# Latent attention: the causal mask and the row maximum of the scores in one VectorE pass per head

## The reference

```python
cq = _rmsnorm(x @ Wq_down, gq)
Q = (cq @ Wq_up).reshape(B, S, H, dh).transpose(0, 2, 1, 3)
Q_nope, Q_rope = (Q[..., :nope], Q[..., nope:])
...
KV_lora = _rmsnorm(KV_lora, gkv)
KV = (KV_lora @ Wkv_up).reshape(B, S, H, dh + nope).transpose(0, 2, 1, 3)
...
mask = jnp.where(jnp.tril(jnp.ones((S, S), jnp.float32)) == 1, 0.0, -1000000000.0)
scale = 1.0 / jnp.sqrt(jnp.float32(q_heads.shape[-1]))
scores = jnp.einsum('bhsd,bhtd->bhst', q_heads, k_heads) * scale + mask
attn = jax.nn.softmax(scores, axis=-1)
out = jnp.einsum('bhst,bhtd->bhsd', attn, V)
out = out.transpose(0, 2, 1, 3).reshape(B, S, D) @ Wo
```

## Time and profile before

| | |
|---|---|
| median of 3 runs | 3078.67 us (3078.39 to 3084.72) |
| the profiled execution | 3087.53 us |
| its span in the trace | 3086.1 us |
| latent stage in it | 0 to about 562 us |
| TensorE busy over the span | 2887.0 us (94%) |
| VectorE busy over the span | 2055.0 us (67%) |
| mean granted TensorE clock | 0.967 of full speed |

### The profile page before, as it was taken

How to read it: one execution, slowest core, us unless ns; L and a number is a source line. 1 busy time by engine, 2 the same in 40 slices (tenths; PEclk the granted TensorE clock), 3 DMA queues, 4 the chain that set the end, 5 groups by cost and what they waited for, 6 DMA issues and landing times.

```text
span 3086.1 us, 46590 instructions
## 1 busy us (share of the span) xinstructions
PE 2887.0 (94%) x16712; PEld 1971.4 (64%) x16745; DVE 2055.0 (67%) x3792; ACT 1595.0 (52%) x2971; POOL 1138.1 (37%) x1152
## 2 busy tenths in 40 slices
PE   8899998899998889999996999999999999989998
PEld 3344443444443548888865888888888888856665
DVE  3554445699986877777776445656555566549998
ACT  2223222288887537777752444444456455437764
POOL 2343243334422033333345445454544444323310
PEclk9899999799999889999997999999999999989999
DMA  3000000000000238865673013222122234120000
GB/s 132 1 1 1 1 1 1 8 6 6 3 2 21 80 139 331 326 247 192 213 222 98 21 32 84 63 57 68 49 90 88 81 115 134 35 89 8 15 15 21
DMA packets 125913, 238.83 MB, mean 77 GB/s; under 512 B 14283, under 2 KB 73248, under 8 KB 119285
## 3 DMA queue, kind: packets, MB, share of 16 engines
q1 hardware_dynamic: 102020, 119.95, 12.1%
q0 software_dynamic: 22512, 113.80, 10.7%
q10 hardware_dynamic: 1152, 2.10, 0.2%
HBM read 223.99 MB, written 40.63 MB: 86 GB/s over the span
## 4 chain that ended last, share of the span: by engine, by line
PE 55%; DVE 13%; issue 7%; ACT 6%; POOL 3%; DMA 1%; SPq 0%; POOLq 0%; ACTq 0%; DVEq 0%; another core or an unknown queue 0%
PE ps L1651 9%; PE ps L1653 9%; PE ps L1652 9%; PE ps L901 3%; PE ps L890 3%; PE ps L2918 2%; DVE ps L2493 2%; PE ps L879 2%; PE ps L2928 2%; DVE b_mx L1023 1%; PE ps L2893 1%; ACT d_PTh L2355 1%; PE ps L1665 1%; ACT d_qk L2340 1%; DVE d_PTl L2507 1%
## 5 line engine op out<-in xcount | busy, mean ns | idle before, releaser
L2693 POOL TENSOR_SCALAR d_P<-d_P,d_rv 128x128 f32<-128x128 f32 (+3 forms) x256 | 289.8, 1144 | 553.2 <-DVE d_rv L2500 552.9
L1023 DVE TENSOR_REDUCE b_mx<-ps 128x1 f32<-128x512 f32 x512 | 320.8, 683 | 31.7 <-PE ps L879 28.1
L964 ACT ACTIVATE b_PT<-ps 128x512 f32<-128x512 f32 x512 | 277.6, 601 | 45.0 <-PE ps L890 43.5
L2348 ACT ACTIVATE d_P<-ps,d_nb 128x128 f32<-128x128 f32 (+3 forms) x256 | 135.2, 528 | 219.0 <-DVE d_nb L2493 217.7
L2507 DVE TENSOR_TENSOR d_PTl<-ps,d_PTh 128x384 fp32r<-128x384 f32 (+1 forms) x192 | 114.6, 597 | 157.4 <-ACT d_PTh L2355 157.4
L1651 PE MATMUL ps<-d_xh,d_wh 128*128 128x512 f32 x512 | 210.1, 410 | 1.5 <-DVE d_xl L2467 1.4
L1652 PE MATMUL ps<-d_xl,d_wh 128*128 128x512 f32 x512 | 204.1, 399 | 0.0
L1653 PE MATMUL ps<-d_xh,d_wl 128*128 128x512 f32 x512 | 203.9, 398 | 0.0
L879 PE MATMUL ps<-b_KT,b_Q 64*128 64x512 f32 x512 | 201.0, 475 | 2.1 <-DVE b_mx L1023 1.0
L890 PE MATMUL ps<-b_Q,b_KT 64*128 64x512 f32 x512 | 187.1, 452 | 0.5
L476 ACT ACTIVATE a_P<-ps 128x2048 f32<-128x2048 f32 (+1 forms) x48 | 76.4, 1592 | 210.0 <-PE ps L340 183.0
(11 more groups left out here) (485 smaller groups left out, 8456.3 us busy)
## 6 DMA issues: line engine op xcount, KB each, us to landing
eoscr<-x_eo SPq DMA_DIRECT2D x87, 256.0 KB, 4.3
d_w<-in_L_attn_W_Q SPq DMA_DIRECT2D x32, 256.0 KB, 3.9
d_w<-in_L_attn_W_K SPq DMA_DIRECT2D x32, 256.0 KB, 4.7
d_w<-in_L_attn_W_V SPq DMA_DIRECT2D x32, 256.0 KB, 5.4
d_wo<-in_L_attn_W_O SPq DMA_DIRECT2D x16, 512.0 KB, 4.7
d_cmb<-in_wgT SPq DMA_DIRECT2D x16, 512.0 KB, 5.0
d_cmb<-in_wuT SPq DMA_DIRECT2D x16, 512.0 KB, 4.7
d_cmb<-in_wdT SPq DMA_DIRECT2D x16, 512.0 KB, 4.2
```

The costliest lines, as they stand in the source:

```text
L964: e.activation(M.PT[:, half, v % 2, 2 * p + y, :], ps[:, O.bank(("ex", v, y)), :], ACT.Exp, scale=0.25).then_inc(S["b_ex"], 1)
L1023: e.tensor_reduce(M.mx[:, r % 2, q, h:h + 1], ps[:, O.SCORES[O.score(t, h) % 3], :], AX.X, ALU.max).then_inc(S["b_mx"], 1)
L2693: e.tensor_scalar(P, P, M.rv[:, y, q:q + 1], None, ALU.mult).then_inc(S["d_nm"], 1)
```

## The change

In `scores` the mask matmuls (L322) are gone, 256 in all; those of `turned` stay. VectorE no longer takes the maximum of four heads by one reduction: for each head and block, one `tensor_tensor_reduce` adds a mask from SBUF (`M.mk`: 384 columns of zero, then the 128x128 mask, so that its last w columns fit a block of w columns), writes the sum back to PSUM and gives the maximum. A group has 16 of them in place of 4 reductions. `M.mk` is filled once at the start, on VectorE. Part 1 now begins with the small block.

```diff
@@ scores
         for q, c0 in (((3, 0),), ((2, 0), (0, 384)), ((1, 0),))[j]:
             w = 128 * (q + 1)
             for i in range(4):
-                e.matmul(ps[:, i, c0:c0 + w], M.QT[32 * i:32 * i + 32, c, q * 128:q * 128 + 128], M.KT[32 * i:32 * i + 32, c, 0:w], start=True, stop=False)
-            for i in range(4):
-                t = e.matmul(ps[:, i, c0 + w - 128:c0 + w], G.identb, G.maskb, start=False, stop=True)
+                t = e.matmul(ps[:, i, c0:c0 + w], M.QT[32 * i:32 * i + 32, c, q * 128:q * 128 + 128], M.KT[32 * i:32 * i + 32, c, 0:w], start=True, stop=True)
         t.then_inc(S["a_S"], 1)
@@ peak
-        if j == 1:
-            e.tensor_reduce(M.mx[:, 0, :], ps[:, 0:4, 384:512], AX.X, ALU.max)
-        q = 3 - j
-        w = 128 * (q + 1)
-        e.tensor_reduce(M.mx[:, q, :], ps[:, 0:4, 0:w], AX.X, ALU.max).then_inc(S["a_mx"], 1)
+        if g == 0 and j == 0:
+            e.wait_ge(S["a_mk"], 2)
+        for q, c0 in (((3, 0),), ((0, 384), (2, 0)), ((1, 0),))[j]:
+            w = 128 * (q + 1)
+            for i in range(4):
+                part = ps[:, i, c0:c0 + w]
+                t = e.tensor_tensor_reduce(out=part, in0=part, in1=M.mk[:, 512 - w:512], scale=1.0, scalar=-3.4e38, op0=ALU.add, op1=ALU.max,
+                                           accum_out=M.mx[:, q, i:i + 1])
+        t.then_inc(S["a_mx"], 1)
@@ latent_dve, at the start
             t.then_inc(S["cb"], 1)
+            e.memset(M.mk[:, 0:384], 0.0).then_inc(S["a_mk"], 1)
+            e.tensor_copy(M.mk[:, 384:512], G.cst[:, C_MASK:C_MASK + 128]).then_inc(S["a_mk"], 1)
```

More of the change, by code:

```diff
@@ L189, in latent_memory @@
     M.rec, M.o = sb("a_rec", [128, 512]), sb("a_o", [128, 4, 512])
+    M.mk = sb("a_mk", [128, 512])
     return M
```

## The result

| | before | after |
|---|---|---|
| median of 6 runs each, taken together | 3084.48 us (3078.39 to 3094.44) | 3096.84 us (3092.36 to 3101.42) |
| ratio to before | | 1.0043, 95% interval 1.0031 to 1.0055 |
| span of the profiled execution | 3086.1 us | 3093.0 us |
| last matmul of the latent stage | 563.0 us | 573.7 us |
| TensorE busy over the span | 2887.0 us | 2881.0 us |

The change makes the kernel slower by 0.43%, about 13 us; 4.8 were forecast. All of it arises in the latent stage, which ends 10.7 us later in the profiled execution. The later stages of that execution gave 3.8 us back, nearly all of it between 2755 and 3069 us (times of the kernel before), where TensorE was equally idle in both (17.7 and 17.8 us) and had 12.9 us at the lower clock instead of 19.9. The last row of the table is summed from the trace's clock records.

What follows compares the result with a forecast made beforehand. The latent stage was taken as bound by the chain of scores, maximum, turned and exponential, not TensorE alone. Chain +0.3 us plus clock 4.5 gave +4.8 on 3078.67, so 3083.5 us, range 3075 to 3085.

Steps and rivals of the forecast that it cites:

- the sum: Latent stage: gains and costs at 45 places where turned follows a maximum, +0.3 us; with 4.5 us for TensorE's clock, +4.8.
- TensorE's clock: Lower clock behind longer idle time before turned, part 1, of groups 5, 9, 13: +4.5 us, ends 0 and 9.
- kind C: 20 places where fill work covers the maximum and turned begins without idle time; the scores' earlier end is won: -7.9 us.
- The price of a pass: VectorE: passes of 512, 384, 256, 128 columns 0.66, 0.53, 0.38, 0.26 us apart; maxima longer by 0.44, 0.90, 0.39 us.
- rival of full reads and tails: Every accumulator read and pass tail on VectorE counts in full: +26 us, with the clock +30, 3109 us; chance 0.13.
- Kind B: Six places, part 1 of groups 3 to 13 (odd), where VectorE starts the maximum late; its added length costs +5.4 us.
- kind A: 17 places where VectorE follows the scores at once and turned follows the maximum at once: +1.9 us.
- m: How much earlier scores end without mask matmuls: 0.33 us in parts 0 and 2, 0.66 us in part 1.
- D: Two places, part 1 of groups 14 and 15, with VectorE and TensorE nearly even: +0.9 us.
- rival of a clock that falls more often: TensorE's clock falls at more than three places and stays low longer: +0.3 + 9 us, 3088 us; chance 0.17.
- period over 134 us: Test on the time of four groups, expected 130 to 132 us; above 134 the price of a pass would be wrong.

Runs made afterwards that it cites:

- e4_settle_behind: Changed kernel with the settling of the group before moved on VectorE from ahead of the maximum of part 1 to behind it: 3077.00 us, ratio 0.9980 to before.
- e7_filler_short: Changed kernel with three unused matmuls on TensorE ahead of turned, part 1, at groups 3, 5, 7, 9, 11, 13: 3086.58 us, ratio 1.0008 to before.
- e13_filler_at_3: Changed kernel with three unused matmuls on TensorE ahead of turned, part 1, at groups 5, 9 and 13 alone: 3090.25 us, ratio 1.0041 to before.
- e3_filler: Changed kernel with six unused matmuls on TensorE ahead of turned, part 1, at groups 3, 5, 7, 9, 11, 13: 3101.96 us, ratio 1.0053 to before.
- e12_before_order: Kernel before with settling behind the maximum of part 1 and tile 2's normalisation ahead of the maximum of part 0: 3072.41 us, ratio 0.9973.
- e6_masks_out_settle_behind: Kernel before without the mask matmuls of scores, four reductions kept, settling behind the maximum of part 1: 3065.22 us, ratio 0.9935.
- e10_all_three: Kernel before without scores' mask matmuls, settling behind the maximum of part 1, tile 2's normalisation ahead of the maximum of part 0: 3058.43 us, ratio 0.9915.
- e2_masks_out: Kernel before without the mask matmuls of scores, its four reductions kept: 3070.73 us, ratio 0.9955.
- e11_after_order: Changed kernel with settling behind the maximum of part 1 and tile 2's normalisation ahead of the maximum of part 0: 3070.02 us, ratio 0.9964 to before.
- e1_passes_only: Changed kernel with the mask matmuls of scores put back, the new VectorE passes kept: 3105.95 us, ratio 1.0064 to before.

## Where the prediction was right and where not

Two terms of the sum failed. TensorE's clock was put at 4.5 us and took about 8 in the traces, and kind C was put at -7.9 us and gave about -4. The price of a pass and what it does where VectorE is late were right.

**The base.** The forecast of 3083.5 stood on the median of three runs, 3078.67 us. In the comparison with the changed kernel the kernel before had 3084.48. Of the 13.3 us between the forecast and the measured 3096.84, 5.8 are this base and 7.5 the difference itself, +12.4 for +4.8.

**The price of a pass, right.** Pitches (distances from start to start) of 0.65, 0.52, 0.38 and 0.25 us for 0.66, 0.53, 0.38 and 0.26. The maxima are longer by 0.41, 0.81 and 0.41 us for 0.44, 0.90 and 0.39. The rival of full reads and tails falls: part 0 would take four times 0.69 + 0.14, 3.32 us, and the trace has 2.70. The Trainium skill (VectorE: DVE Perf Modes, section "The DRAIN you can't avoid"), from which the prediction took that the next operation waits until the pipe is empty, adds in the same paragraph that an operation which is not held back starts earlier. The trace agrees with this addition: the passes start 0.65 us apart, beside the read of the one before.

**Kind B and most of kind A, right.** Turned waits in 25 places. The gaps at groups 5, 9 and 13 are 2.99 us for 3.0, with some luck: to the 1.45 us come 0.73 for the masks and 0.81 for the maximum, where 0.66 and 0.90 stood. At group 5 the start of turned moves by 0.81 us against the scores, for 0.90. Part 0 of kind A moves by 0.10 us for 0.11, but part 1 (groups 4, 8 and 12) by -0.15 for +0.24. TensorE's busy time is 115.8 for about 115, VectorE's 68.1 for 70.5. The period was missed: 133.5 us, and 130 to 132 were expected.

**Kind C, partly wrong.** "Covered by fill work" was read from TensorE alone. In part 0 of groups 2, 6 and 10 the fill work itself waits for VectorE, behind the maximum. TensorE in group 6, first a row of the kernel before, then the changed kernel:

```profile
234.43 0.63 PE L238 MATMUL ps<-cst,a_xn 128*128 128x128 f32 x4 [2.26 <-DVE a_xn L94]
```

```profile
232.24 0.61 PE L239 MATMUL ps<-cst,a_xn 128*128 128x128 f32 x4
235.39 0.63 PE L239 MATMUL ps<-cst,a_xn 128*128 128x128 f32 x4 [2.54 <-DVE a_xn L94]
235.95 1.36 PE L335 MATMUL ps<-a_QT,a_KT 32*128 32x512 f32 x8
...
237.67 0.61 PE L339 MATMUL ps<-cb 128*128 128x128 bf16 x4
```

and VectorE, where L94 starts as the last head's maximum is read:

```profile
234.06 0.73 DVE L572 CUSTOM_DVE_ANT_0 ps<-ps,a_mk 128x512 f32<-128x512 f32 x1
234.71 0.14 DVE L572 DVE_READ_ACCUMULATOR2_ANT a_mx<- 128x1 f32 x1
234.71 1.00 DVE L94 TENSOR_SCALAR a_xn<-X,mv,rs 128x512 f32<-128x512 f32 x2
```

These places do not gain 0.33 us: the way from the scores to turned is 0.06 us longer at groups 6 and 10.

Where kind C did hold, its places with one block of scores gave less than m = 0.33 us. A row of four masks takes 0.33 us from start to start only ahead of a product; ahead of fill work it takes 0.23, as in group 7, part 2, of the kernel before:

```profile
289.27 0.40 PE L322 MATMUL ps<-cb 128*128 128x128 bf16 x4
289.50 2.80 PE L283 MATMUL ps<-a_kv,a_wkn 128*128 128x512 f32 x6
```

The 64 rows together take 17.6 us and not 21. In the changed kernel turned moves up there by 0.19 us, and by 0.20 in part 0 of groups 4, 8 and 12; part 1 gave 0.73 for 0.66. Read place by place over groups 1 to 15, the way from the scores to turned has become 2.7 us longer in all, where the sum had +0.3 (up to 1 us of it, either way, is clock). Kind C as a whole gave about 4 us for 7.9; kinds A, B and D cost 1.3 us less than they were put at, which made part of that good.

**TensorE's clock, the term that was mis-sized.** The sum took 4.5 us, three places of 1.5. (Its pattern, group 7, was well chosen; group 11, named beside it, has only 2.23 us of idle time.) The new low stretches at groups 5, 9 and 13 came as told, 1.46, 1.46 and 1.93 us. What it did not have: group 3, low twice as long for another 1.2 us, and part 0 of groups 6 and 10, where 2.54 us of idle time (2.26 before) led to 0.61 us mask matmuls, 1.58 us each. These six add up to 9.2 us. At other places low stretches of the kernel before became shorter or moved, so the way from turned to the next scores is 8.2 us longer in all, between groups 1 and 15, of which 0.6 is no clock (0.2 each behind part 2 of groups 4, 8 and 12). With the 2.7 us of the chain that is 10.9; less 1.7 us that this execution was ahead at group 1, and with 1.4 behind group 15, where the clock is lower again, the stage's +10.7 us is accounted for, by rows of one pair of traces.

That is the size of the prediction's rival of a clock that falls more often, which had a chance of 0.17; but that rival looked for further falls where kind A gets longer and at groups 3, 7 and 11, and only group 3 is among these. It had not looked where fill work stands idle. What happened there is in part chance: behind the same 2.54 to 2.55 us the clock fell at groups 6 and 10 in two other kernels (e4_settle_behind, e7_filler_short), at group 6 alone in e13_filler_at_3, and at neither in e3_filler.

**The point from which a verdict hangs.** The prediction said that a period over 134 us would speak against the price of a pass. It is 133.5, and the passes are as priced to 0.01 us; a period mixes the chain and the clock, so this test could not have told them apart. The pitch and the 0.61 us rows could, and did.

**What stays open.** The time at the lower clock differs between executions of the same code by 11 us within the first 140 us (15.9 in the changed kernel, 27.3 in e13_filler_at_3, where nothing differs up to there). So the figure for the clock, about 8 us, is its cost in one pair of traces. That the clock behind idle time costs the changed kernel about 11 us rests on the short filler's ratio (1.0043 to 1.0008, intervals apart). How much of that the change added is shown by the rows of the places only, and the filler at three places alone did not confirm a total.

## What to carry over

When an engine is waited for, look at what stands ahead of the awaited work in its own list: here two changes of VectorE's order took 8 us from the median of the kernel before (14.8 us from the stage in the profile, which had a better clock), while taking 17.6 us of mask matmuls from TensorE at the price of longer maxima cost 12 us. Follow a wait one step further than the engine that stands idle: "covered by fill work" holds only where the fill work does not wait for the same engine. In this kernel, price an idle time of 2.7 us and more on TensorE at its length plus about 1.5 us of lower clock (up to 2.8 where the stretch was twice as long), and one of 2.2 us at half of that; expect that the number of such places varies from run to run, so compare such kernels by many runs and not by two traces.

## What the runs showed of the hardware

- A read of the accumulator has 0.14 us alone, but adds only 0.04 to 0.05 us between two passes of one line, in runs of four and eight (pitches 0.65 and 0.25 us, above).
- Idle time of TensorE before turned, part 1, at the odd groups 3 to 13, and the clock behind it: after 1.42 to 1.53 us full speed at 12 of 12 places (before, e12_before_order, e6_masks_out_settle_behind, e10_all_three); after 2.18 to 2.26 us lower at 6 of 13 (2.18 in e2_masks_out, one of three; 2.23 in before, one of one; 2.23 in e4_settle_behind, one of three; 2.23 in e11_after_order, two of three; 2.26 in e1_passes_only, one of three); after 2.69 to 4.41 us lower at 23 of 23, among them the 2.99 us of the changed kernel. A small change of an idle time can so cost more than itself.
- Matmuls whose result nobody reads, in idle time of TensorE, took the changed kernel from 1.0043 to 1.0008 of the kernel before when they ended before the awaited maximum (2.84 us of them), and to 1.0053 when they ended behind it (5.42 us).
